# First stage of a Fourier attention block: two groups of images pulled ahead of the statistics, small products spread between groups, GpSimd on the weights, stores on SyncE's queue

## What is computed

```
x = x + L0(group_norm(x))          # attention over images, with spectral convolutions
x = x + L1(group_norm(x))          # one wide spectral convolution

# L0, start:
xn = instance_norm(x)                                   # per image
k, q, v = fourier_layer(xn, Kcw|Qcw|Vcw, Ksw|Qsw|Vsw)   # 32 heads: spectrum * weights + skip
...                                                     # attention, p = fourier_layer(av, Pcw, Psw)
```

## Time and profile before

| | us |
|---|---|
| runs before | 1078.45 median of 3 (1077.09 to 1087.74) |
| the profiled execution, its own time | 1081.58 |
| its span, first to last instruction | 1079.9 |
| first block, to the start of the second block's work | 117.0 |
| second block, up to the softmax's end | about 70 |

### The profile page before, as it was taken

One profiled execution on the slowest core, in us unless ns is written; L12 is line 12 of the kernel. 1 busy time (PEld: TensorE's weight loads), 2 busy tenths in 40 slices (PEclk: granted clock), 3 DMA queues, 4 the chain that ended last, 5 costly groups with the idle time before them and its releaser, 6 DMA issues. The chain is left out here.

```text
span 1079.9 us, 36766 instructions
## 1 busy us (share of the span) xinstructions
PE 802.2 (74%) x16050; PEld 588.2 (54%) x16050; DVE 682.8 (63%) x1459; ACT 403.6 (37%) x914; POOL 368.1 (34%) x262
## 2 busy tenths in 40 slices
PE   0499494699999954999923999467777777776797
PEld 0365241122222224888813999467666766666686
DVE  4897498478888885466658899635544544453132
ACT  0298342022222245555533566333333332332121
POOL 0022472589999910111100000324444444442000
PEclk9999697599999976999955999789888888888899
DMA  9566620494556430354231566579999999999587
GB/s 364 111 188 158 149 46 0 146 335 154 192 168 195 130 88 6 95 178 115 57 72 39 159 193 183 126 157 265 266 266 266 264 269 261 269 262 188 167 254 214
DMA packets 270191, 189.40 MB, mean 175 GB/s; under 512 B 29252, under 2 KB 259365, under 8 KB 268901
## 3 DMA queue, kind: packets, MB, share of 16 engines
q1 hardware_dynamic: 189571, 131.51, 45.9%
q10 hardware_dynamic: 75426, 44.17, 17.1%
q0 software_dynamic: 5120, 12.75, 4.2%
HBM read 154.48 MB, written 33.07 MB: 174 GB/s over the span
## 5 line engine op out<-in xcount | busy, mean ns | idle before, releaser
L2007 PE MATMUL po<-pa,room 128*32 128x16 f32 x8320 | 146.9, 221 | 85.4 <-DMA room<-_L_conv_weight_imag_dram 55.9
L2007 PEld LDWEIGHTS po<-pa,room 128*32 128x32 f32 x8320 | 144.4, 163 | 93.1 <-issue 61.1
L982 POOL TENSOR_TENSOR q<-wb,xb 128x1536 f32<-128x1536 f32 (+1 forms) x51 | 170.4, 3365 | 42.1 <-DMA wb<-wv 30.5
L1052 DVE TENSOR_TENSOR q<-pw,xb 128x1536 f32<-128x1536 f32 (+1 forms) x85 | 140.8, 1704 | 25.7 <-PE acc L1022 15.5
L1022 PE MATMUL acc<-q,pt 128*32 128x384 f32 (+1 forms) x1088 | 104.4, 496 | 15.3 <-DVE q L1052 15.3
L2148 DVE TENSOR_TENSOR osl<-po,neg 128x128 f32<-128x128 f32 x64 | 18.4, 288 | 150.3 <-ACT neg L2081 150.3
L1960 POOL DMA_DIRECT2D os_<-osl x64 | 45.4, 715 | 183.0 <-DVE osl L2159 175.0
L1950 POOL COPY cols<-y 128x512 f32<-128x512 f32 x32 | 38.3, 1196 | 147.7 <-POOLq L1716 142.0
L2081 ACT ACTIVATE neg<-po 128x272 f32<-128x272 f32 x32 | 12.7, 397 | 197.3 <-issue 182.6
L1994 PE MATMUL px<-wbat,cols 128*32 128x130 f32 x2176 | 75.8, 291 | 4.3 <-DVE wbat L2119 3.0
L1022 PEld LDWEIGHTS acc<-q,pt 128*32 128x32 f32 x1088 | 27.8, 110 | 91.1 <-issue 57.5
(11 more groups left out here) (334 smaller groups left out, 1586.2 us busy)
## 6 DMA issues: line engine op xcount, KB each, us to landing
room<-_L_conv_weight_real_dram ACTq DMA_DIRECT2D x32, 520.0 KB, 9.9
room<-_L_conv_weight_imag_dram ACTq DMA_DIRECT2D x32, 520.0 KB, 12.6
room<-_L_conv_weight_real_dram SPq DMA_DIRECT2D x32, 520.0 KB, 7.0
room<-_L_conv_weight_imag_dram SPq DMA_DIRECT2D x32, 520.0 KB, 10.6
xb<-xns SPq DMA_DIRECT2D x64, 192.0 KB, 3.2
wb<-wv SPq DMA_DIRECT2D x16, 576.0 KB, 5.9
yall<-in_x_dram SPq DMA_DIRECT2D x4, 2048.0 KB, 14.4
xd<-in_x_dram SPq DMA_DIRECT2D x16, 512.0 KB, 4.3
```

What stands on the lines that cost most here:

```text
L982: nc.gpsimd.tensor_tensor(q2[:, t % 2, :, :, 0:m], bc(weights(blk, n), 2, NB), spectra(blk), ALU.mult).then_inc(s_qp, 1)
L1052: V.tensor_tensor(q1[:, t % 2, :, :, 0:m], bc(pw[t % 4][:, 0:3 * m].rearrange("p (r m) -> p r m", r=3), 2, NB), spectra(blk), ALU.mult).th ...
L2007: e = nc.tensor.matmul(po[u][32 * g:32 * g + 32, 512 * q + 16 * m:512 * q + 16 * m + 16], wsl[u][:, :, q * KWF + KWF - 1 - kw], xsl[u][:, ...
```

## The change

- TensorE does the height transforms of groups 0 and 1 before it waits for the statistics. The products for the group moments and for `rt` come after group 1's height transform, the three sets of weight products after those of groups 2, 3 and 4.
- ScalarE waits for `rt` and starts with group 0's copy. The second root (alpha) is served after group 0's normalising.
- VectorE computes alpha and beta first and then the weight columns. The clearing of `vf`, the two copies into `pr`, the product `pr[1]*vf[1]` and the scaling of `vf` go to GpSimd, with new semaphores between the two.
- The stores of the spectra go from GpSimd's to SyncE's queue, between the loads. Batch 1 is reloaded after store 10, batch 2 after store 14, batch 0 before store 15, batch 3 after it.
- TensorE's second batch of groups is written out too, so only the last two are in a loop.

```diff
 SyncE
+                for g in range(GPB):
+                    load(g)
+                for g in range(NGRP):
+                    if g + GPB < NGRP:
+                        sp.wait_ge(s_f1, g + 1)
+                        load(g + GPB)
+                    if g >= 2:
+                        store(g - 2)
...
+                    if g == 12:
+                        spectra_back(1)
+                store(NGRP - 2)
+                spectra_back(2)
                 sp.wait_ge(s_wt, 1)
                 spectra_back(0)
+                store(NGRP - 1)
                 spectra_back(NB - 1)
 GpSimd
+                nc.gpsimd.memset(vf[:, :, :, :], 0.0).then_inc(s_vf, 1)
+                pool.wait_ge(s_w, 16 * NW)
+                for r in range(2):
+                    nc.gpsimd.tensor_copy(pr[:, r], praw[:, :, :, r].rearrange("n h w -> n w h")).then_inc(s_pr, 1)
+                pool.wait_ge(s_p1, 1)
+                nc.gpsimd.tensor_tensor(pr[:, 1], pr[:, 1], vf[:, 1], ALU.mult).then_inc(s_wp, 1)
+                pool.wait_ge(s_p0, 1)
+                pool.wait_ge(s_wp, 1)
+                nc.gpsimd.tensor_scalar(vf[:, :, :, :], vf[:, :, :, :], hs[:, 3:4], None, ALU.mult).then_inc(s_vs, 1)
 ScalarE
-                act.wait_ge(s_rts, 1)
-                root.serve(act, nc.scalar, v1("alpha"))
...
+                        if g == 0:
+                            root.serve(act, nc.scalar, v1("alpha"))
 TensorE
+                between = {1: group_moments, 2: conv_weights, 3: weight_columns, 4: columns_symmetrised}
...
+                        if isinstance(b, int) and g in between:
+                            between[g]()
 VectorE
-                V.memset(vf[:, :, :, :], 0.0)
-                for r in range(2):
-                    s = V.tensor_copy(pr[:, r], praw[:, :, :, r].rearrange("n h w -> n w h"))
...
-                ch.link(V.tensor_tensor(pr[:, 1], pr[:, 1], vf[:, 1], ALU.mult))
-                ch.link(V.tensor_tensor(wt[:, 0], wt[:, 0], pr[:, 1], ALU.subtract))
                 ch.link(V.tensor_tensor(wt[:, 1], wt[:, 1], pr[:, 0], ALU.add))
-                ch.link(V.tensor_scalar(vf[:, :, :, :], vf[:, :, :, :], psk, None, ALU.mult))
+                dve.wait_ge(s_wp, 1)
+                ch.link(V.tensor_tensor(wt[:, 0], wt[:, 0], pr[:, 1], ALU.subtract))
+                dve.wait_ge(s_vs, 1)
```

More of the change, by code:

```diff
@@ L362, in _, with load, store @@
                     sp.dma_start(xa[:, i * n:(i + 1) * n], xf[:, i * n:(i + 1) * n]).then_inc(s_x[i // 2], 16)
[L364 to L372, removed]
+                def load(g):
+                    sp.dma_start(xd[:, g % GPB, :].rearrange("h (g w) -> h g w", g=GI),
+                                 x[g * GI:g * GI + GI].rearrange("g h w -> h g w")).then_inc(s_xd[g % GPB], 16)
+                def store(g):
+                    sp.wait_ge(s_e2, g + 1)
+                    sp.dma_start(xs[g * GI:g * GI + GI].rearrange("i m k -> m i k"), xst[:, g % 2]).then_inc(s_xs[g % 2], 16)
                 def spectra_back(b):
@@ L432, in _ @@
                 act.wait_ge(s_rw, 1)
+                act.wait_ge(s_rts, 1)
                 def copy(b):
@@ L458, in _ @@
                 pe.wait_ge(s_const, 16 * (len(kept) + len(SCALARS)))
[L459 to L466, removed]
@@ L480, in _, with group_moments @@
[L480 to L484, removed]
+                def group_moments():
+                    pe.wait_ge(s_me, 1)
+                    nc.tensor.matmul(pg[:, 0:2 * NG], bmean[:, :], me[:, :, :].rearrange("p a g -> p (a g)"),
+                                     start=True, stop=True).then_inc(s_gm, 1)
+                    pe.wait_ge(s_rw, 1)
+                    for i in range(2):
+                        m = nc.tensor.matmul(pg[:, 128 + 4 * i:132 + 4 * i], rw[:, i, :], sel[:, :],
+                                             start=True, stop=True)
+                    m.then_inc(s_rt, 1)
@@ new lines, in conv_weights, with weight_columns @@
+                def conv_weights():
+                    pe.wait_ge(s_mst, 32)
+                    for i in range(2):
+                        for r in range(2):
+                            o = 64 * (2 * i + r)
+                            m = nc.tensor.matmul(pw[64:64 + KW, o:o + 64], mst[:, i, :, r], ident[64:128, 64:128], start=True, stop=True)
+                    m.then_inc(s_mtp, 1)
+                def weight_columns():
+                    pe.wait_ge(s_col, 1)
+                    pe.wait_ge(s_mtr, 1)
+                    for i in range(3):
+                        m = nc.tensor.transpose(pw[0:2 * RH, 32 * i:32 * i + 32],
+                                                col[:, i].rearrange("n r h -> n (r h)"), ident[0:NHD, 0:NHD])
+                    m.then_inc(s_ct, 1)
@@ L508, in transform @@
                             w_transform(b - 1, GPB - 1)
-                per_batch(pe, transform)
+                for b in range(2):
+                    transform(b)
+                with pe.Fori(2, NB) as b:
+                    transform(b)
                 w_transform(NB - 1, GPB - 1)
@@ L573, in _ @@
                 ch.link(V.tensor_tensor(v1("beta"), scalar["norm1_b"], v1("beta"), ALU.subtract))
+                dve.wait_ge(s_w, 16 * NW)
+                kv = [kvq[:, i, :].rearrange("n (h w r) -> n r w h", h=RH, w=RW) for i in range(3)]
+                for i in range(3):
+                    s = V.tensor_copy(col[:, i], kv[i][:, :, 0, :])
+                s.then_inc(s_col, 1)
                 for i in range(2):
```

57 lines of the change are left out of this document (22 added, 35 removed).

## The result

The changed kernel took 1085.28 us as the median of 20 runs, against 1081.41 for the kernel before in 20 runs: a ratio of 1.0043, with a 95% interval of 1.0028 to 1.0058. It is slower by 0.4%: the medians differ by 3.9 us, and the ratio amounts to 4.6. The forecast was 1077.5 and the range 1072.5 to 1081, so it lies outside. The forecast was built on a median of three runs of the kernel before, 1078.45; over 20 runs that kernel takes 3.0 more. This explains 3.0 of the 7.8 us that the forecast is off, and the change itself the other 4.8: 3.9 lost where 0.9 was to be gained. The profiled execution of the changed kernel took 1084.88 us, 3.3 more than that of before.

The account below looks back on a forecast made before the run. TensorE was taken to bound the first stage's middle: 5.8 us gained, 1.5 and 2.5 lost, then the tail of stores and reloads starts the second block 0.9 us earlier. From 1078.45 it forecast 1077.5, range 1072.5 to 1081.

Parts of the forecast that it names:

- Two height transforms ahead of the statistics: First-stage start: transforms from 33.6 to 40.1, moments 2.3 us late, yet first width transform 5.8 us earlier, at 45.9.
- Weight products in the stream, 1.5: TensorE's first-stage stream: 17 weight matmuls, now in the critical part, cost 1.5 us.
- The clock, 2.5: TensorE, nearly idle between 40.1 and 45.9, falls to its lower clock; the first groups in the stream pay 2.5 us.
- Alpha: First block: computing alpha later costs nothing, since only VectorE's own list and the second block wait for it.
- GpSimd's product and scaling, worth nothing: First-block value weights: moving this work from VectorE gains nothing at the second block, since the tail covers it.
- The 4 us of cover: First-block end: VectorE's last weight product ends at 99.3, reload 0 isn't issued before 103.3, leaving 4 us spare.
- The tail: First-block end: store 15 lands with two reloads at 111.0; the last reload follows and lands at 116.0.
- The sum: Second block's work starts at 116.0 instead of 116.9, 0.9 us earlier; total 1077.5.
- Rival 3: Value weights become last: GpSimd and VectorE disturb each other, both need 30% more from 44 on; 1081.5, chance 0.05.
- the two signs of being wrong: First-block end: last reload issued by 108, or VectorE's last weight product ending after 103.
- rival 1: Store 15 passes the reloads (3 us), or TensorE keeps its upper clock (2.5 us); 1072 to 1075, chance 0.32.
- Rival 2: First-stage start: constants land after 34.5, delaying transforms and moments; landing at 37.8 gives 1081.7; chance 0.15.

Follow-up runs that it names:

- e1: Changed kernel with GpSimd's two copies into `pr` waiting until VectorE has made alpha, beta and the columns: 1077.29 us, ratio 0.9960 to the kernel before.
- e9: e5 with a separate semaphore for the constant matrices, so TensorE doesn't wait for the ten scalars: 1073.99 us, ratio 0.9935 to the kernel before.
- e3: Changed kernel with the `xd` loads of groups 4 and 5 held back until the scales are copied: one run of 1083.59 us.
- e2: Changed kernel with copies, product and scaling back on VectorE, GpSimd keeping only the clearing: 1079.36 us, ratio 0.9980 to the kernel before.
- e4: e1 with the product and the scaling back on VectorE, only the two copies on GpSimd: 1076.68 us, ratio 0.9950 to the kernel before.
- e5: e4 with batch 0 reloaded after store 12 and batch 2 after store 13, ahead of stores 14 and 15: 1071.85 us, ratio 0.9919.
- e8: e2 with six useless 32x2112 copies on GpSimd, on partitions and a tile VectorE doesn't use then: one run, 1081.91 us.

## Why the prediction was wrong

**The step that failed.** The prediction let GpSimd's two copies "run from about 43 to 53 while VectorE is elsewhere" and priced them at nothing. VectorE was not elsewhere: it was making the scales, in the middle of the critical path, and there it was held up for two copies of 4.1. `rt`, forecast at 44.4, came at 52.4, and the first width transform, forecast at 45.9, at 54.2. With nothing but the copies moved out of the way (e1) they come at 44.3 and 46.0, and the second block 8.0 earlier. The sum had missed it by 7.2 (123.2 for 116.0).

**Two height transforms ahead of the statistics.** Forecast: begin at 33.6, moments at 40.1. Measured: 34.22 and 40.80. The constants decide the start, as said; e9 shows it. The prediction put their 0.20 a pass down to the lower level of the clock. The granted clock reads 1.00 there, as it does from 0 on, while TensorE had done nothing. Yet in e9 a height transform at a granted 0.50 ran at the same pace (4 to 5 passes touched in each half microsecond) and went up to 7 when 1.00 was granted. So the durations speak for the lower level, and the record of the clock doesn't show it at this place.

**Weight products in the stream, 1.5.** Measured from the gaps that they make between transforms (59.42 to 59.99, 63.63 to 63.84, 67.49 to 68.05): 1.3. Right.

**The clock, 2.5.** It did fall, to a granted 0.50 during the wait: the first width transform took 3.50 instead of 1.88, but only this one, and behind it the granted clock is 1.00. The loss is 1.6. The term was 0.9 too large.

**Alpha.** The prediction says that "nothing waits for alpha but VectorE's own list and the second block". ScalarE does, since it has alpha's root in its list between the copies of groups 0 and 1. It cost nothing where VectorE came in time, and 6.68 of ScalarE's time in e3.

**GpSimd's product and scaling, worth nothing.** On the value weights themselves they cost much: from the start of the first one 27.3 us before, 37.3 in the changed kernel (75.69 to 113.0). The product costs 4.4 more and the scaling 10.4, where 4.8 is saved. The scaling had been bounded by 9.4 beside VectorE's work; it takes 10.8 and stops VectorE. The 4 us of cover were used up, and the reload of batch 0 went out 2.5 late, with the value weights. But at the second block this cost next to nothing (e1 has both and starts it at 115.17, e2 has neither and starts it at 115.43), as store 15 landed sooner with only one reload just ahead of it. The term was right there by a compensation that the prediction didn't have, which is luck.

**The tail.** Forecast: store 15 lands 8 us after the first of the two reloads is issued. e4 has 101.58 and 109.28, 7.7. Right, and this wait was there to be had: e5 takes it out.

**The sum.** Without GpSimd's share (e2) the last height transform ends at 99.2, forecast 99.1, and the second block starts at 115.43, forecast 116.0. So one error decides, with a price of 7.8 (e2) to 8.0 us (e1) at that point. The small ones cancel: the stream began some 0.5 late in e2, and the clock cost 1.9 there instead of 2.5.

**The rivals.** Rival 3 named the place but put the price at 30% and the time from 44 on, with a chance of 0.05, and its 1081.5 lay outside the range that was to take in most of it. One of the two signs of being wrong came, the last weight product after 103 (113.0), by its mechanism. The argument against it rested on the product of the earlier trace rows, "made while VectorE worked too". Beside it the kernel before has these:

```profile
118.62 0.72 DVE L845 TENSOR_TENSOR xr<-room 128x544 f32<-128x544 f32 x1
119.27 0.71 DVE L846 COPY xr<-room 128x544 f32<-128x544 f32 x1
119.90 0.71 DVE L847 COPY xr<-room 128x544 f32<-128x544 f32 x1
```

GpSimd's product ran from 119.14 to 123.86. Only the last 0.2 of a VectorE product fell into it, then two copies that took no longer than that product, and after them VectorE idled until 123.3. It could not bound the case of two products. The long stage has products on both engines at once, GpSimd's with two inputs in SBUF and VectorE's L1080 with one in PSUM. Taken by shape, L1080 needs 1751 ns for 1536 elements, 1.14 ns each, near the 1.11 of the 2.35 for 2112 (the 1704 above is a mean over two shapes). That shows only that an input in PSUM escapes. No row of the prediction showed two SBUF products on both engines, and the range had no bound from that side. Of rival 1 neither part occurred: store 15 landed with the reloads (e4), and the clock fell. e5 gets the first part's gain by another order. Rival 2 began at 34.5, and the constants were there at 34.2.

The total's part that came back, 3 us in the last long stage, isn't explained. Over the eleven profiles here the time behind the start of the second block lies between 959.5 and 965.4, and the changed kernel is at the short end with 959.9, before at 962.9.

The rule in the Trainium skill (GPSIMD Engine Reference, Key points) says that GpSimd shares its SBUF interfaces with VectorE and contends with VectorE instructions in a two-port mode or with two SBUF inputs. The stalls agree for the products with two SBUF inputs (3.43 and 4.03 in e3, 3.98 in e8), and so does the copy out of PSUM that passed (0.17). L569, L570 and the copy into `vf` have one input; whether they ran in a two-port mode no view shows. The wait was for a whole instruction of the other engine.

## What to carry to other kernels

Work given to GpSimd isn't beside VectorE if VectorE works on SBUF at the time. In these runs VectorE's products with both inputs in SBUF, and some of its copies and `tensor_scalar`s, waited out each GpSimd instruction, and a short one in a critical chain waited as long as a long one. Put GpSimd's long instructions where VectorE reads PSUM or where nothing critical waits for it, and tie them there with a semaphore; when they may start is as much part of the change as what they do. In the profile, look for a VectorE instruction that takes many times its usual length and ends with one of GpSimd's. When stores and large reloads meet, put the reloads that are ready early ahead of the last stores' time, not just before the last store.

## What the runs showed of the hardware

- A VectorE product of 32x2112 with both inputs in SBUF took 3.98 us beside GpSimd's copies and 2.35 alone, though they touched other partitions and another tile (e8). 32-element products took 3.43 and 4.03 (e3), a `tensor_scalar` on 32 elements 3.99, a copy of 128 elements 4.08 (changed kernel), a copy of 32x512 1.63 instead of 0.6 (e1). Not held up were copies out of PSUM (0.17 in e3; 0.43 and 0.25 in e1) and the `kq` copies of 32x544 at 2.0 ns an element (4.43 for four against 4.35).
- GpSimd waits in its turn: its product took 6.83, begun 2.3 before a VectorE product ended, and 4.72 in the earlier trace rows.
- A strided copy of 32x2112 takes 4.1 us on GpSimd, as on VectorE (4.0). Its scaling of 4224 elements takes some 10.8 once VectorE's product has ended (12.87 in all), 4.5 times VectorE's 2.41 (e2).
- A store of 132 KB on SyncE's queue had landed within 2.6 us with the nearest reload of 528 KB issued 3.9 before it (e5), within 4.7 with one reload just ahead (e1), and within 6.8 behind two (e4). On GpSimd's queue stores took 5.7 and 5.1 beside two reloads in flight and 3.3 without (kernel before).
- In the changed kernel TensorE's granted clock was 0.50 from 43.8 to 57.4, most of which it spent waiting, and four passes of the width transform took 3.50 us instead of the 1.88 at 1.00.
